# Query and key heads turned in square blocks by VectorE, put in place by the stores, instead of by TensorE

## The reference, cut to what matters

```
q = (x @ Wq.T).reshape(64, 32, 32, 128)      # 32 query heads of 128
k = (x @ Wk.T).reshape(64, 32, 8, 128)       # 8 key heads
v = (x @ Wv.T).reshape(64, 32, 8, 128)
q, k = rope(rmsnorm(q, q_norm_w)), rope(rmsnorm(k, k_norm_w))
# keys and values of 16 cached pages of 32, and the 32 new ones, masked by length
o = softmax(q @ k_all.T * SCALE) @ v_all
x = x + o @ Wo.T
# then three more residual layers: mixture of experts (rank 16), two slot-selected low-rank layers
```

## Time and profile before

| | |
|---|---|
| median of 3 runs | 2438.04 us (2437.64 to 2438.17) |
| profiled execution: time, span of its instructions | 2440.32 us, 2438.5 us |
| mean granted TensorE clock | 0.996 of full speed |
| first to last scaling of query and key tiles | 60.47 us to 593.06 us |
| first scores of attention | 633.55 us |
| busy share of the span | PE 98%, VectorE 58%, ScalarE 56%, GpSimd 32% |

### The profile page before, as it was taken

How to read it: one execution, slowest core, us unless ns; L and a number is a source line. 1 busy time by engine, 2 the same in 40 slices (tenths; PEclk the granted TensorE clock), 3 DMA queues, 4 the chain that set the end, 5 groups by cost and what they waited for, 6 DMA issues and landing times.

```text
span 2438.5 us, 48070 instructions
## 1 busy us (share of the span) xinstructions
PE 2395.5 (98%) x14960; PEld 2060.7 (85%) x14960; DVE 1418.3 (58%) x3834; ACT 1365.0 (56%) x3340; POOL 769.9 (32%) x852
## 2 busy tenths in 40 slices
PE   8999999999999999999999999999999999999998
PEld 7877777777888989989999999999998788888886
DVE  5777777775366666666666666666665443443333
ACT  4777777776466666666666666666666222222221
POOL 5666666665122233332222222222222101111111
PEclk9999999999999999999999999999999999999999
DMA  5233332323998988998989999998886233333331
GB/s 207 71 115 100 92 104 87 104 87 116 327 343 286 286 282 286 287 288 283 293 282 299 292 291 288 286 296 289 293 289 231 83 99 102 100 106 93 101 104 46
DMA packets 390749, 488.55 MB, mean 200 GB/s; under 512 B 53536, under 2 KB 325152, under 8 KB 387616
## 3 DMA queue, kind: packets, MB, share of 16 engines
q1 hardware_dynamic: 353696, 351.89, 46.0%
q0 software_dynamic: 36864, 134.23, 16.5%
HBM read 397.89 MB, written 88.08 MB: 199 GB/s over the span
## 4 chain that ended last, share of the span: by engine, by line
PE 69%; POOL 10%; issue 8%; ACT 4%; DVE 4%; SPq 3%; DMA 2%; POOLq 0%; DVEq 0%; ACTq 0%
PE s_bank L1008 18%; PE o_bank L1020 16%; PE pt L1055 8%; POOL q_t L498 7%; PE proj L1502 4%; PE proj L1504 4%; PE proj L1503 4%; ACT normed L562 3%; POOL w_hi L458 2%; PE o_bank L1036 2%; POOL w_lo L460 1%; PE acc L728 1%; DVE probs L977 1%; PE acc L729 1%; PE acc L730 1%
## 5 line engine op out<-in xcount | busy, mean ns | idle before, releaser
L977 DVE CUSTOM_DVE_ANT_0 probs<-s_bank,mask 128x544 f32<-128x544 f32 x512 | 371.0, 725 | 428.6 <-PE s_bank L1008 427.9
L932 ACT ACTIVATE probs<-probs,neg_max 128x544 f32<-128x544 f32 x512 | 383.9, 750 | 407.9 <-DVE neg_max L977 407.9
L1008 PE MATMUL s_bank<-k_t,q_t 128*128 128x288 f32 (+1 forms) x2048 | 557.3, 395 | 6.7 <-DVE neg_max L977 2.5
L1020 PEld LDWEIGHTS o_bank<-p_t,v_c 128*128 128x128 f32 x4096 | 527.5, 192 | 29.2
L1020 PE MATMUL o_bank<-p_t,v_c 128*128 128x128 f32 x4096 | 540.0, 275 | 0.0
L1008 PEld LDWEIGHTS s_bank<-k_t,q_t 128*128 128x128 f32 x2048 | 349.1, 190 | 67.8 <-DVE neg_max L977 11.1
L138 POOL DMA_INDIRECT v_c<-in_v_rows,v_row x256 | 255.4, 998 | 301.2 <-PE o_bank L1020 260.6
L728 PE MATMUL acc<-w_hi,x_hi 128*128 128x512 f32 x764 | 314.9, 412 | 0.0
L1055 PE MATMUL pt<-ident,probs 128*128 128x128 f32 x2048 | 310.8, 274 | 0.0
L498 POOL TENSOR_TENSOR q_t<-normed,v_c 128x256 f32<-128x256 f32 x320 | 248.8, 798 | 182.3 <-ACT normed L562 180.3
L904 ACT ACTIVATE p_t<-pt 128x512 f32<-128x512 f32 x512 | 295.8, 578 | 10.3 <-PE pt L1055 1.2
(11 more groups left out here) (154 smaller groups left out, 3440.2 us busy)
## 6 DMA issues: line engine op xcount, KB each, us to landing
k_t<-in_k_pages SPq DMA_DIRECT2D x1024, 128.0 KB
q_spill<-wo_early SPq DMA_DIRECT2D x32, 1024.0 KB, 5.2
q_t<-q_spill SPq DMA_DIRECT2D x64, 512.0 KB
o_spill<-o_t SPq DMA_DIRECT2D x64, 512.0 KB, 5.2
raw<-o_spill SPq DMA_DIRECT2D x64, 512.0 KB, 3.5
k_t<-in_w_qkv SPq DMA_DIRECT2D x11, 1024.0 KB, 8.1
v_spill<-wo_early SPq DMA_DIRECT2D x8, 1024.0 KB, 7.2
k_spill<-wo_early SPq DMA_DIRECT2D x8, 1024.0 KB, 5.1
```

The lines of the kernel that those rows point to most:

```text
L932: nc.scalar.activation(probs[:, j % SLOTS_P], probs[:, j % SLOTS_P], ACT.Exp, scale=-1.0, bias=neg_max[:, j % 2:j % 2 + 1], accum_out=row_ ...
L977: nc.vector.tensor_tensor_reduce(out=probs[:, j % SLOTS_P], in0=s_run, in1=mask[:, par], scale=-SCALE, scalar=3.0e38, op0=ALU.add, op1=ALU ...
L1008: last = pe.matmul(s_bank[:, columns].rearrange("p (s t) -> p s t", t=PSIZE), q_t[:, par, g], k_t[:, par, slots, g], start=True, stop=True)
L1020: last = pe.matmul(o_of(n), v_c[:, par, c, g * HD:(g + 1) * HD], p_t[:, i, c], start=g < QUAD and c == 0, stop=False)
```

## The change

TensorE's transposes and ScalarE's copies out of `flip` go. VectorE turns each roped tile of 128 tokens by 512 columns in square blocks of 32, 4 by 16 of them (each block by itself, within its 32 partitions) and writes the result into the stage. Partitions then hold, for each of the four sequences, 32 values of a head's index, instead of all 128; the stores put the blocks in place: one for each tile and sequence, 32 partitions by four runs of 512 bytes, so 16 transfers of 64 KB per group where one of 1 MB was. In VectorE's iteration n, `turn(n-2)` comes last, behind `total(n)`. The two `flip` banks of PSUM become accumulators: six instead of four. Waits that counted `flipped` or one store per group are changed to count `staged_qk` and the new number of stores.

```diff
-    MM_BANKS = 4
+    MM_BANKS = 6
...
-        flip = [ctx.enter_context(nc.psum_tensor(f"flip{i}", [P, SLICE], F32)) for i in range(2)]
...
+        def stored_before(g):
+            return 16 * sum(1 if KIND[i // GROUPS] == "v" else QUARTER * TB for i in range(g % 2, g, 2))
...
                 else:
-                    sp.wait_ge(staged_qk, qk_before(last))
                     to, at = (q_dram, i * HS * S) if KIND[s] == "q" else (k_dram, (i - NQ) * HS * S)
-                    dst = to[g * QUARTER * TB:(g + 1) * QUARTER * TB, :, at:at + HS * S]
-                    sp.dma_start(dst.rearrange("b d n -> d b n"),
-                                 buf.rearrange("p (b n) -> p b n", n=HS * S)).then_inc(stored[g % 2], 16)
+                    for t in range(QUARTER):
+                        sp.wait_ge(staged_qk, qk_before(last - QUARTER + t + 1))
+                        for a in range(TB):
+                            dst = to[(g * QUARTER + t) * TB + a, :, at:at + HS * S].rearrange("(c e) n -> e c n", e=S)
+                            src = buf[a * S:(a + 1) * S, t * SLICE:(t + 1) * SLICE].rearrange("p (c n) -> p c n", n=HS * S)
+                            sp.dma_start(dst, src).then_inc(stored[g % 2], 16)
...
-            for n in range(TILES + 4):
-                if is_qk(n - 4):
-                    stage_turned(n - 4)
+            for n in range(TILES + 1):
...
                 if is_qk(n):
+                    if n == NT:
+                        act.wait_ge(trig_done, 2)
                     square(n)
...
-                at_least(dve, flipped, m - 1)
+                at_least(dve, staged_qk, m - 1)
                 nc.vector.tensor_tensor(roped[:, i], part_s[:, :, :], part_c[:, i], ALU.add)\
                     .then_inc(roped_done, 1)
+
+            def turn(n):
+                m, i = qk_before(n), n % 2
+                dve.wait_ge(roped_done, m + 1)
+                if n % QUARTER == 0:
+                    at_least(dve, stored[group_of(n) % 2], stored_before(group_of(n)))
+                nc.vector.transpose(stage_of(n).rearrange("p (c h s) -> p h c s", h=HS, s=S),
+                                    roped[:, i].rearrange("p h (c e) -> p h c e", e=S)).then_inc(staged_qk, 1)
...
                     total(n)
+                if is_qk(n - 2):
+                    turn(n - 2)
...
-            def turn(n):
-                m, i = qk_before(n), n % 2
-                pe.wait_ge(roped_done, m + 1)
-                at_least(pe, staged_qk, m - 1)
-                for h in range(HS):
-                    last = pe.transpose(flip[i][:, h * P:(h + 1) * P], roped[:, i, h], ident[:, :])
-                last.then_inc(flipped, 1)
...
                 multiply(n)
-                if is_qk(n - 3):
-                    turn(n - 3)
```

More of the change, by code:

```diff
@@ L336, in project @@
         roped_done = sem("roped_done")
-        flipped = sem("flipped")
         staged_qk = sem("staged_qk")
@@ L359, in group_of, with stage_of @@
             return n // QUARTER
+        def stage_of(n):
+            t = n % QUARTER
+            return stage[:, group_of(n) % 2, t * SLICE:(t + 1) * SLICE]
+        def stored_before(g):
+            return 16 * sum(1 if KIND[i // GROUPS] == "v" else QUARTER * TB for i in range(g % 2, g, 2))
         def w_landed(engine, s):
@@ L397, in first_batch @@
                     for i in range(2):
-                        sp.wait_ge(stored[i], 16 * (NSL - 1) * GROUPS // 2)
+                        sp.wait_ge(stored[i], stored_before((NSL - 1) * GROUPS + i))
                     sp.wait_ge(x_split, len(PIECES))
-                    sp.wait_ge(flipped, QKS)
+                    sp.wait_ge(staged_qk, QKS)
                     sp.wait_ge(tables_k, 4)
@@ L510, in _ @@
             for i in range(2):
-                pool.wait_ge(stored[i], 16 * (NSL - 1) * GROUPS // 2)
+                pool.wait_ge(stored[i], stored_before((NSL - 1) * GROUPS + i))
             for par in range(2):
@@ L535, in wait_stage @@
                     g = group_of(n)
[L536 to L547, removed]
+                    at_least(act, stored[g % 2], stored_before(g))
             def stage_values(n):
@@ L854, in _ @@
             for i in range(2):
-                sp.wait_ge(stored[i], 16 * NSL * (NT // QUARTER) // 2)
+                sp.wait_ge(stored[i], 16 * (NV + (NQ + NK) * NT) * (NT // QUARTER) // 2)
             sp.wait_ge(projected, NSL * NT)
```

## The result

The changed kernel takes 2493.18 us, the median of 4 runs (2490.91 to 2495.72), against 2437.84 us before (four runs): 1.0228 times the time, 95% interval 1.0214 to 1.0241. The prediction was 2502, slower with a chance of 0.91. The profiled execution took 2490.91 us with a span of 2489.1, the shortest of the four; the one before had a span of 2438.5.

| part | before | after | measured | predicted |
|---|---|---|---|---|
| start to first scaling | 60.47 | 60.04 | -0.4 | 0 |
| 159 steps of the query and key tiles | 532.6 | 590.4 | +57.8 | +67 |
| last scaling to first scores | 40.5 | 36.3 | -4.2 | -3 |
| scores to the end | 1805.0 | 1802.3 | -2.6 | 0 |

What follows compares the result with a forecast made beforehand. A VectorE-ScalarE ring of 3.32 us per tile, not TensorE, was taken as the bound. Steps of 3.66 us plus 18 for splits gave +67, the end -3: 2438 + 64 = 2502 us, range 2470 to 2590.

Steps and rivals of the forecast that it cites:

- the ring: Query and key tiles: scaling, squares, total, go_straight, reciprocal, once per tile across ScalarE and VectorE, without slack; 3.32 us per step.
- The transpose on the ring, +0.60: VectorE's turn, between total and go_straight, takes one pass and adds 0.60 us to each query and key step.
- Rival C: VectorE's transpose takes two passes: +0.56 us per step, 2591 us; chance 0.10.
- go_straight, -0.26: Behind turn, go_straight starts after GpSimd's cross is over, takes 0.69 us and gives back 0.26 per step.
- Rival B: go_straight stays slowed since GpSimd shifts along: step 3.92 us, 2535 us; chance 0.10.
- Split tiles, +18: In 40 tiles GpSimd's weight splitting falls under go_straight and delays the next cross: 0.45 us each, 18 us.
- The stores, 0: Sixteen 64 KB stores per group on SP, 2.0 to 2.6 us per 3.66 us step, stay hidden.
- Rival D: The small stores become the bound: at 1.0 us per issue the step is 4.0 us, 2556 us; chance 0.05.
- The end, -3: From last scaling to first scores: scores start at about 37.5 us instead of 40.5; bounds 0 and -9.
- The chain named in the prediction: Stretch's end: last value tiles wait for a stage half whose store stands on SP behind the first batch's loads.
- rival E: TensorE's clock falls as TensorE idles 0.9 us per step: 2502 to 2560 us; chance 0.04.
- The signs: Expected in the trace: ScalarE idle before scaling some 1.6 us, TensorE idle 0.9 us per step for a drained accumulator.

Runs made afterwards that it cites:

- the ring shortened: Kernel before the change, VectorE reordered to total(n), reciprocal(n), go_straight(n-1), add(n-1), with no VectorE transpose: 2419.39 us, 0.9925.

## Why the prediction was right, step by step

- **The bound.** TensorE's 98% was not the bound; the ring was. Shown from both sides: without TensorE's transposes the kernel before doesn't move (1.0002), and with them in addition the changed one doesn't (1.0240 against 1.0228). But the prediction read too much room from the earlier trace rows: its 35.7 us add waits of weight loads to waits of matmuls, of which the first lie largely beside running matmuls. PE idled for 8.5 us in the whole stretch, and with the ring shortened TensorE's own step was 3.22 us against 3.33: 0.1 us of room per step, enough for the ring to be the bound and no more.
- **The transpose on the ring, +0.60.** It lasts 0.70 us and the next instruction starts 0.62 after it, one pass. Moved into idle time it costs nothing (0.9993). The other estimate in the prediction, 0.71 us, fits as well. Rival C (two passes) is out.
- **go_straight, -0.26.** It lasts 0.65 and from its start to the reciprocal's it takes 0.57, not 0.60: -0.29 against the 0.86 before. With the transpose's 0.62 that is again 3.66, the step as predicted. Shown by the order that puts it back into cross: 3.92 us. Rival B is out for this order, and right for that one.
- **Split tiles, +18: the term that was mis-sized.** Measured 590.4 - 159 x 3.66 = 8.5 us, 0.21 each instead of 0.45. The cast took 0.61 us instead of 1.08, since it now starts beside the transpose (218.46) and not inside go_straight; go_straight meets only the cast, ends 0.55 us behind it and is slowed by 0.19, not 0.34; the subtraction falls on add (1.64 us), whose slack just holds it; the step behind a split isn't touched. The stretch came out 9.2 us short of the forecast, the median 8.7 us (2493.18 against 2502): the split tiles are the main part of that, while the smaller differences of the table lie within the scatter of the runs.
- **The stores, 0.** Right (1.0237). Rival D is out. The warning about merging small transfers (the Trainium skill, DMA: Bandwidth & Descriptors, rules for kernel authors) didn't bite: the trace has 640 of 64 KB, the size at which that rule's overhead begins, landing in 1.8 us each (median), off every path.
- **The end, -3.** -4.2. The chain named in the prediction is what held it: ScalarE waited 13.2 us for a stage half. Freeing it showed the queries' landing right behind, which the prediction didn't have. Six accumulators contribute under 1 us.
- **TensorE's clock (rival E).** It fell, to 0.96 on average in the stretch, and cost nothing there: with four accumulators it stayed at 1.00 and the stretch was as long. It didn't fall for the reason given, some idle time in every step; see below.
- **The signs.** Two came out otherwise. ScalarE's idle time ahead of the scaling grew from 0.65 to 0.98 us, not to 1.6, because another 0.75 us of waiting lies ahead of its square root. TensorE idled for a drained accumulator in 80 of some 140 steps, not in each.

The 2.6 us after the scores stay unexplained. They are within the scatter: that part took 1802.3 to 1809.5 us in the thirteen profiles here.

## What to carry to other kernels

An engine that is 98% busy need not be the bound: look for a ring between engines in which each instruction starts at the end of the one before, and read the step from it. Work added to an engine that is busy for only 58% costs its full length if its place in the program order is on that ring, and nothing a few lines further up, where the engine idled; before moving work to an engine, write down the order around it and what each place would delay. And price a moved instruction together with its neighbours: what runs at its new time on an engine that it has to take turns with, as VectorE does with GpSimd here.

## What the runs showed of the hardware

- **VectorE and GpSimd in turns.** A VectorE instruction with two inputs from SBUF waits for the GpSimd one that is running: add, 0.69 us alone, started at 219.65 beside the subtraction of 219.15 to 220.74 and lasted 1.64, to 0.55 us behind its end. The 0.55 us is the same wherever it was looked at: go_straight ends 0.55 us behind cross and behind the cast (219.62 against 219.07). In the profile before the change all 200 two-input VectorE instructions of the stretch that start while a GpSimd one runs end 0.54 to 0.55 us behind it, and the other 120 last 0.69 us. So the price of such a meeting can be worked out: the rest of GpSimd's instruction and 0.55 us, instead of 0.69. Transpose (0.70) and reduce (0.69) with one input ran beside cross and the cast at full speed, and beside the subtraction too, in the run with the transpose off the ring (0.71). The Trainium skill (SBUF — State Buffer, Terms) calls the pair of ports that the two share a lock held for a whole instruction; these rows agree. It works the other way too: GpSimd's cast takes 0.61 here and took 1.08 when it started beside go_straight.
- **The granted clock.** The changed kernel's TensorE waits up to 0.9 us for an accumulator in many steps, but in the stretch its clock falls ten times, each time in or right behind a wait of 3.3 to 4.4 us, for weights at the start of a slice. The windows around one (columns as above):

```profile
216.00:219.00 3.00, 0.48 (x3) 0.05 (x1) 1.94 (x4) 1.82 (x6) 1.89 (x3) 1.00 0.37 87
219.00:222.00 3.00, 1.21 (x4) 0.96 (x5) 2.89 (x4) 1.63 (x5) 2.70 (x4) 0.87 0.37 87
222.00:224.00 2.00, 2.00 (x6) 1.55 (x5) 2.00 (x5) 0.89 (x4) 0.58 (x1) 0.50 0.15 37
224.00:226.00 2.00, 2.00 (x9) 1.63 (x8) 0.94 (x3) 1.25 (x5) 1.38 (x2) 0.84 0.41 98
```

  0.50 is 1.2 GHz of 2.4. With four accumulators TensorE isn't far enough ahead to have that wait. It waits in each of 140 steps instead, 0.67 us on average, its busy time in the stretch is the same to 2%, and the clock is 1.00 throughout (the window of the stretch, and the waits from 120 to 640 us):

```profile
60.00:650.00 590.00, 487.39 (x1929) 350.04 (x1928) 459.64 (x792) 306.44 (x954) 323.47 (x398) 1.00 0.34 86
```

```profile
PE acc L735 <- ACT normed L559: 93.9, 140, 0.9
```

  The time is the same, since TensorE catches up inside its slack. A low clock isn't free where the matmuls are in the chain: TensorE idles 4.07 us ahead of the first scores of attention, these run at 0.50 and are 3.0 us apart (686.79, 689.88, 692.88), against 2.0 in the kernel before, and the first outputs come 13.2 us behind the first scores instead of 9.1. That is some 4 us, as much as the earlier end of the stage had won. Whether it lasts to the end of the kernel isn't shown, since the part behind the scores scatters by more.
